# An attention kernel whose TensorE order is written out as letters, with idle products in its opening

## The chip, the cores and the metric

The kernel runs on one core of one Trainium2 chip. The metric is the device time of one execution in microseconds (us), the median of three runs.

## The reference, cut to what matters

A macaron block in float32: half a mixture of eight experts, attention, and half a mixture again, over x of 4 batches x 1024 tokens x 128 features.

```python
x = x + 0.5 * _L0_ffn_ref(_layernorm(x), Wr, br, ln_g, ln_b, W1, b1, W2, b2)
x = x + _L0_attn_ref(_layernorm(x), Wq, Wk, Wv, Wo)
x = x + 0.5 * _L0_ffn_ref(_layernorm(x), Wr, br, ln_g, ln_b, W1, b1, W2, b2)


# inside _L0_attn_ref: 16 heads of 8 features
q = split_heads(x @ Wq.T); k = split_heads(x @ Wk.T); v = split_heads(x @ Wv.T)
q = _rope(q, pos); k = _rope(k, pos)
score = jnp.einsum('bqd,bkd->bqk', q, k)
score = jnp.where(causal[None], score, -jnp.inf)
attn = jax.nn.softmax(score / jnp.sqrt(jnp.float32(D_K)), axis=-1)
out = jnp.einsum('bqk,bkd->bqd', attn, v)
return out @ Wo.T
```

## The kernel before, in words

**Stages.** Attention works in 16 stages (NST) of four heads (QH) of one batch. Queries and keys are split into three bf16 parts each and stacked, so that one product over 72 rows gives a float32 score. Each stage is done twice over: first the row maxima are found, then the scores are computed again with the maximum subtracted, through three more rows of the stack (75 rows), and exponentiated.

**The jobs on TensorE.** Each has a function.
- `tile` (L1297): scores of 128 queries against all keys up to them, into one of two PSUM buffers `psS`. There are 24 per stage: t0 to t7 hold two heads (128, 256, 384, 512 columns a head; two tiles of each), t8 to t23 one head (640, 1024, 768 and 896 columns, four of each, in this order). VectorE (`reduce`, L1448) adds the mask and takes the maximum. They are made for the stage after the one whose scores run.
- `turn_max`: turns the split maxima of one half of a stage (half 0: queries 0 to 511, the first eight tiles; half 1: the rest). GpSimd splits them before (`split`, five short steps), VectorE copies the result (`copy_max`, L1456), a DMA writes it into the stack (`load_max`).
- `score` (L1339): scores turned, of 128 keys against up to 512 queries, into one of three PSUM buffers `psST`. A stage has 12 units (u0 to u11) of four heads (s4.0 is unit 4, head 0; w4 is its weigh), of 512, 384, 256, 128, five times 512, 384, 256, 128 queries, 48 scores in all. Scores of unit 4 and later need the maxima of half 1. ScalarE's `exps` (L1412) takes the exponential.
- `weigh` (L1353): the exponentials of one unit times the values, into `psO`; for units on the diagonal GpSimd's `mask` (L1533) stands before it. ScalarE copies `psO` after units 3 and 11 (`copy_out`, L1418).
- `turn_out` (L1323): turns such a copy back, and VectorE divides by the sums (`normalise`).

**What waits for what.** The jobs `tile`, `turn_max` and `turn_out` take turns on the two buffers of `psS`: each is a use with an index, and use k waits until VectorE has read use k-2 (`use`: `wait(pe, use_read, index - 1)`). Score m waits for exponential m-3. `exps` of unit u waits for weigh u-3, since `prob` is a ring of three. In the last stage there are no tiles, and the scores use five buffers.

**The order.** TensorE works its queue in order. `plan(first, last)` computes the order of a stage: scores in order, a weigh two units behind (LAG = 2) after the first score of each unit, tiles spread by cost (`spread`), and the turns at fixed units (EXTRAS). Before the stages stands `opening()`: 12 tiles of stage 0, its first `turn_max`, four more tiles, and eight tiles with the 16 scores and 2 weighs of units 0 to 3 among them. Written with the letters that the change uses (s score, w weigh, t tile of the next stage, o tile of stage 0 in the opening, m and M the turn of half 0, N of half 1, A and B `turn_out` of half 0 and 1), the order before is:

```
opening  oooooooooooomooooossossossosssowsossoswosss
first    tttNwtttttwtssstsstsstsAswtsstsswtstssMswttsstsswtstssswtsstsswtsss
middle   swttsstsswtsstsNswtssstswssstswtssstBswtsstsAswtsstsswtstssMswttsstsswtstssswtsstsswtsss
last     swsssswsssNswsssswsssswsssBswsssAswsssswsssswsssswsssswsssswssswwB
```

VectorE and GpSimd follow the same list of uses (`uses`, `base`, `half_ready`). Ahead of attention TensorE runs products of ones (`warm_up`, L253).

Of the kernel before, what the change touches and what calls it, by code (L numbers as in the profile page):

```python
# [20 lines left out]
P = 128  # L21
# [8 lines left out]
QH = 4  # L30
# [1065 lines left out]
def attention(nc, n, ctx, block):  # L1096
# [26 lines left out]
    tile_cost = [len(heads) * (i + 1) * P + 350 for heads, i in tiles]  # L1123
    tile_total = sum(tile_cost)

    WEIGH_COST = 3
    att_total = sum((QH + WEIGH_COST) * w for _, _, _, w in units)

    def plan(first, last, whole=False):

        found, tile = [], 0
        att = sum((QH + WEIGH_COST) * w for _, _, _, w in units[:OPEN]) if first and not whole else 0

        def spread():
            nonlocal tile
            while not last and tile < MT and sum(tile_cost[:tile + 1]) * att_total <= att * tile_total + AHEAD:
                found.append(("tile", tile, 0))
                tile += 1  # L1140

        if first and not whole:
            found += [("tile", t, 0) for t in range(OPEN_TILES)]
            tile = OPEN_TILES
        for u in range(UN):
            if first and not whole and u == OPEN:
                for v in range(OPEN - LAG, OPEN):
                    found.append(("weigh", v, 0))
                    att += WEIGH_COST * units[v][3]
                    spread()  # L1150
            w = units[u][3]
            for h in range(0 if first and u < OPEN and not whole else QH):
                found.append(("score", u, h))
                att += w
                if h == 0:
                    if u >= (OPEN + LAG if first and not whole else LAG):
                        found.append(("weigh", u - LAG, 0))
                        att += WEIGH_COST * units[u - LAG][3]
                    elif u < LAG and not first:
                        found.append(("weigh", u - LAG, 1))  # L1160
                        att += WEIGH_COST * units[u - LAG + UN][3]
                spread()
            for at, what, arg, there in EXTRAS:
                if at == u and (there or not (first if arg == 1 and what == "turn_out" else last)):
                    found.append((what, arg, 0))
        att = att_total * 2
        spread()
        return found

    OPEN, OPEN_AFTER, OPEN_TILES = CB, 4, 3  # L1170

    def opening():

        head = MT // 2 + 1 + OPEN_AFTER
        found = [(what, arg, 0) for _, what, arg in before_loop[:head]]
        jobs = plan(True, True, True)
        jobs = jobs[:jobs.index(("score", OPEN, 0))]
        jobs = [job for job in jobs if job[0] in ("score", "weigh")]
        for k, (_, what, arg) in enumerate(before_loop[head:]):
            found.append((what, arg, 0))  # L1180
            a, b = (len(jobs) * i // (MT - MT // 2 - OPEN_AFTER) for i in (k, k + 1))
            found += jobs[a:b]
        return found

    def uses(first, last):

        return [(0, what, arg) for what, arg, _ in plan(first, last) if what in ("tile", "turn_max", "turn_out")]

    LAG = 2
    AHEAD = tile_total * tile_cost[0]  # L1190

    EXTRAS = [(1, "turn_max", 1, True), (4, "turn_out", 1, False), (5, "turn_out", 0, True),
              (7, "turn_max", 0, False)]
    before_loop = [(0, "tile", t) for t in range(MT // 2)] + [(0, "turn_max", 0)]
    before_loop += [(0, "tile", t) for t in range(MT // 2, MT)]
    OPENED = [arg for what, arg, _ in opening() if what == "weigh"]
    USES = len(uses(False, False))

    def base(s, first):

        return len(before_loop) if first else len(before_loop) + len(uses(True, False)) + (s - 1) * USES

    PARITY = base(1, False) % 2
    assert USES % 2 == 0

# [43 lines left out]
    def run(stage):  # L1249


        stage(0, 0, 0, True, False)
        for s in range(1, NST):
            stage(s, s % RING, s // RING, False, s == NST - 1)
# [8 lines left out]
    def _(sp):  # L1263
# [10 lines left out]
        def stage(s, r, turn, first, last):  # L1274
            if not first:
                load_max(s, r, 1)
            if not first and s + 2 < NST:
                load(s + 2, (r + 2) % RING)
            if not last:
                load_max(s + 1, (r + 1) % RING, 0)  # L1280
# [11 lines left out]
    def _(pe):  # L1292
# [4 lines left out]
        def tile(r, turn, t, index, ps):  # L1297

            heads, i = tiles[t]
            if t == 0:  # L1300
                pe.wait_ge(stack_loaded[r], (turn + 1) * 16 * STACK_DMAS)
# [24 lines left out]
        def score(s, r, u, h):  # L1326

            ch, j, q0, w = units[u]
            if u in half_start and h == 0:
# [5 lines left out]
            elif m < 5:  # L1335
                pe.wait_ge(use_read, base(s, False))
# [5 lines left out]
        def weigh(s, r, u):  # L1342

            ch, j, q0, w = units[u]
            pe.wait_ge(exp_done, s * SC + (u + 1) * QH)
# [12 lines left out]
        def stage(s, r, turn, first, last):  # L1358
            b, parity = base(s, first), base(0, True) % 2 if first else PARITY
            k = 0  # L1360
            for what, arg, arg2 in plan(first, last):
                if what == "score":
                    score(s, r, arg, arg2)
                    continue
                if what == "weigh":
                    if arg2:
                        weigh(s - 1, (r - 1) % RING, arg + UN)
                    else:
                        weigh(s, r, arg)
                    continue  # L1370
                ps = psS[(parity + k) % 2]
                if what == "tile":
                    tile((r + 1) % RING, turn + (r + 1) // RING, arg, b + k, ps)
                elif what == "turn_max":
                    turn_max(s if arg else s + 1, arg, b + k, ps)
                else:
                    turn_out(s - 1 if arg else s, arg, b + k, ps)
# [8 lines left out]
        k = 0  # L1386
        for what, arg, arg2 in opening():
            if what == "score":
                score(0, 0, arg, arg2)
            elif what == "weigh":  # L1390
                weigh(0, 0, arg)
            elif what == "tile":
                tile(0, 0, arg, k, psS[k % 2])
# [198 lines left out]
```

## Time and profile before

| what | value |
|---|---|
| runs | 857.47, 857.72, 861.70 us, median 857.72 |
| profiled execution, span | 855.6 us from its first to its last instruction |
| profiled execution, own time | not listed apart from the three runs; the median lies 2.1 us above the span |
| TensorE busy | 779.7 us (91%) |
| VectorE busy | 610.9 us (71%) |
| ScalarE busy | 507.4 us (59%) |
| GpSimd busy | 315.4 us (37%) |
| mean granted TensorE clock | 0.945 of full |

Times in the rows are counted from the start of the span. PE is TensorE, DVE VectorE, ACT ScalarE, POOL GpSimd. A product's shown duration reaches past the start of the next product, so how long one occupies the engine is read from start to start. PEclk is the granted clock as a share of 2.4 GHz; 0.50 is 1.2 GHz. Attention runs from about 202 to 714 us.

### The profile page before, as it was taken

The numbers are of one execution on the slowest core, as the hardware profiler recorded it, in microseconds if no ns is written. First come the engines' busy times: TensorE is split into PE (matmuls) and PEld (weight loads), VectorE is DVE, ScalarE is ACT, GpSimd is POOL, SyncE is SP. The second block draws the span as 40 slices with busy tenths as digits, with TensorE's granted clock in tenths as the row PEclk, the third lists the DMA queues.
The fourth block names the chain that finished last, engine by engine and source line by source line (L and its number), as shares of the span: only waits on it lengthen the run. The fifth ranks groups of instructions, "written<-read, shape, count | busy, mean of one in ns | idle before, by whom it ended". The sixth has DMA issues, their size and how long they took to land. (4 is left out here: it accounts for less than half of the span.)

```text
span 855.6 us, 17846 instructions
## 1 busy us (share of the span) xinstructions
PE 779.7 (91%) x5570; PEld 427.9 (50%) x5570; DVE 610.9 (71%) x1919; ACT 507.4 (59%) x1229; POOL 315.4 (37%) x603
## 2 busy tenths in 40 slices
PE   9889999887899999999999999999999997689995
PEld 8888896543233333333333333333333335579884
DVE  4657774698668777788878878788787722856663
ACT  2166651673247767667667766766777684146662
POOL 6177742475104223223322422331242231056753
PEclk8699999998569999999999999999999998789998
DMA  8721113065332033033113303312320001122110
GB/s 271 270 57 50 54 33 117 23 169 159 57 57 45 14 57 57 10 49 58 34 26 57 53 6 57 58 22 36 57 41 18 3 1 34 73 70 50 52 42 26
DMA packets 27989, 51.84 MB, mean 61 GB/s; under 512 B 7552, under 2 KB 19200, under 8 KB 26496
## 3 DMA queue, kind: packets, MB, share of 16 engines
q1 hardware_dynamic: 21296, 41.04, 20.7%
q0 software_dynamic: 4096, 8.69, 3.8%
q10 hardware_dynamic: 2512, 1.06, 0.5%
q8 instruction: 43, 0.70, 0.4%
q14 instruction: 42, 0.34, 0.1%
HBM read 35.40 MB, written 14.97 MB: 59 GB/s over the span
## 5 line engine op out<-in xcount | busy, mean ns | idle before, releaser
L1448 DVE CUSTOM_DVE_ANT_0 cst<-psS,mask_row 128x768 bf16<-128x768 f32 (+7 forms) x512 | 364.7, 756 | 100.2 <-PE psS L1308 97.6
L1412 ACT ACTIVATE prob<-psST 128x512 f32<-128x512 f32 (+3 forms) x750 | 317.3, 495 | 158.9 <-PE psST L1339 155.2
L1353 PE MATMUL a_psO<-prob,vs 128*32 128x512 f32 (+3 forms) x1536 | 166.7, 506 | 2.8 <-ACT prob L1412 1.7
L1532 POOL TENSOR_TENSOR a_gate<-a_zeros 1x1 f32<-1x1 f32 x128 | 23.7, 185 | 333.7 <-ACT prob L1412 333.7
L1339 PE MATMUL psST<-a_qs,ks 75*128 75x512 bf16 (+1 forms) x480 | 123.7, 327 | 5.9 <-ACT prob L1412 3.5
L1308 PE MATMUL psS<-ks,a_qs 72*128 72x512 bf16 (+2 forms) x480 | 119.0, 337 | 5.6 <-DVE a_rowmax L1448 5.5
L777 POOL DMA_INDIRECT tok<-rows,f_there_number x64 | 61.8, 966 | 86.0 <-DVE f_number L489 42.0
L1308 PEld LDWEIGHTS psS<-ks,a_qs 72*128 72x128 bf16 x480 | 35.6, 99 | 101.1 <-DVE a_rowmax L1448 33.0
L1308 PE MATMUL psS<-ks,qs 72*128 72x512 bf16 (+3 forms) x288 | 75.8, 354 | 6.7 <-DVE a_rowmax L1448 6.5
L1533 POOL TENSOR_SCALAR_AFFINE_SELECT prob<-prob 128x512 f32<-128x512 f32 x128 | 80.3, 627 | 0.0
L1339 PE MATMUL psST<-qs,ks 75*128 75x512 bf16 (+3 forms) x270 | 73.4, 346 | 2.7 <-ACT prob L1412 1.7
L1339 PEld LDWEIGHTS psST<-a_qs,ks 75*128 75x128 bf16 x480 | 43.8, 97 | 61.4 <-ACT prob L1412 28.8
L726 ACT ACTIVATE f_xnT<-f_ps_half,gb 128x128 f32<-128x128 f32 x64 | 29.3, 458 | 54.4 <-PE f_ps_half L654 54.4
L522 DVE TENSOR_SCALAR f_hidT<-f_ps_wide,f_w1s 128x128 f32<-128x128 f32 x156 | 47.2, 345 | 18.0 <-PE f_ps_logit L663 13.7
L663 PE MATMUL f_ps_wide<-f_xnT,f_w1s 128*128 x312 | 49.7, 282 | 10.0 <-ACT f_hidT L734 5.4
L743 ACT ACTIVATE f_w1s<-w 128x516 f32 x78 | 49.7, 637 | 9.8 <-DVE f_item_ring L479 9.3
L1353 PEld LDWEIGHTS a_psO<-prob,vs 128*32 128x32 f32 x1536 | 30.6, 108 | 48.1 <-ACT prob L1412 31.6
L1308 PEld LDWEIGHTS psS<-ks,qs 72*128 72x128 bf16 x288 | 21.6, 100 | 64.5 <-DVE a_rowmax L1448 28.4
L663 PEld LDWEIGHTS f_ps_wide<-f_xnT,f_w1s 128*128 128x128 f32 x312 | 40.9, 191 | 14.1 <-issue 14.0
L673 PE MATMUL f_ps_rank<-w,f_hidT 128*128 x320 | 45.4, 285 | 0.3 <-DVE f_hidT L522 0.3
L1339 PEld LDWEIGHTS psST<-qs,ks 75*128 75x128 bf16 x270 | 25.6, 102 | 38.8 <-ACT prob L1412 17.9
L1448 DVE DVE_READ_ACCUMULATOR2_ANT a_rowmax<- 128x1 f32 x512 | 42.6, 83 | 0.0
(183 smaller groups left out, 1066.1 us busy)
## 6 DMA issues: line engine op xcount, KB each, us to landing
a_qs<-q_split SPq DMA_DIRECT2D x60, 96.0 KB
rows<-tok SPq DMA_DIRECT2D x8, 536.0 KB, 4.9
ks<-k_split SPq DMA_DIRECT2D x32, 128.0 KB
qs<-q_split SPq DMA_DIRECT2D x36, 96.0 KB
q_split<-p_part SPq DMA_DIRECT2D x24, 128.0 KB, 2.4
k_split<-p_part SPq DMA_DIRECT2D x24, 128.0 KB, 2.4
ks<-k_split SPq DMA_DIRECT2D x16, 192.0 KB
tok<-x_after_first SPq DMA_DIRECT2D x4, 536.0 KB, 5.4
```

Of the source, the lines that this page charges most:

```text
L522: last = nc.vector.tensor_scalar(hidT[i % 2][:, f * P:(f + 1) * P], hidden_at(i, f), w1s[i % 4][:, F + f:F + f + 1], 0.0, ALU.add, ALU.max)
L663: last = nc.tensor.matmul(hidden_at(i, f), w1s[i % 4][:, f * P:(f + 1) * P], xnT[:, ds(slot_of[i], 1), :], start=True, stop=True)
L673: last = nc.tensor.matmul(psY[i % 2], hidT[i % 2][:, f * P:(f + 1) * P], n.w2[:, ds(expert[i], 1), f * D:(f + 1) * D], start=(f == 0), sto ...
L726: nc.scalar.activation(xnT[:, t % XR, :], psX[t % 2], ACT.Identity, bias=n.gb[:, 1:2], scale=n.gb[:, 0:1]).then_inc(x_ready, 1)
L743: nc.scalar.activation(w1s[i % 4][:, :], n.w1[:, ds(expert[i], 1), :], ACT.Copy).then_inc(w1_ready, 1)
L777: pool.indirect_dma_start(out=row[:, t, :], out_offset=None, in_=n.rows_dram[r][:, :], in_offset=bass.IndirectOffsetOnAxis(ap=there_number ...
L1308: last = nc.tensor.matmul(ps[:, a * CH + c0:a * CH + c0 + w], lhs, ks[r][0:PR, h * S + c0:h * S + c0 + w], start=True, stop=True)
L1339: nc.tensor.matmul(score_buffer(s, m)[:, 0:w], ks[r][:, h * S + j * P:h * S + (j + 1) * P], qs[r][:, q_col(h, q0):q_col(h, q0) + w], start ...
L1353: last = nc.tensor.matmul(psO[32 * h:32 * h + 32, c0:c0 + w], vs[r][:, j, h, :], prob[:, u % RING, h, 0:w], start=(j == 0), stop=(u + 1 in ...
L1412: nc.scalar.activation(prob[:, u % RING, h, 0:w], score_buffer(s, u * QH + h)[:, 0:w], ACT.Exp, scale=SCALE).then_inc(exp_done, 1)
L1448: last = nc.vector.tensor_tensor_reduce(out=out[:, a * CH:a * CH + width], in0=ps[:, a * CH:a * CH + width], in1=mask_row[:, S - width:], ...
L1533: nc.gpsimd.affine_select(out=part, in_=part, compare_op=ALU.is_ge, fill=0.0, base=0, pattern=[[0, QH], [1, P]], channel_multiplier=-1).th ...
```

## The change

`plan`, `opening`, `uses` with its cases for first and last, `before_loop` and the tail behind `run` go away. The order is three strings, one for the first, the middle and the last stage; `jobs(s)` turns letters into jobs by counting them, and all engines read their order from the same `program`. The opening is now part of the first string. New is the letter `f`: an idle product of ones, 128 rows by 512 columns, into `psO`, whose content nothing reads. There are 48, all among the 24 tiles `o` of the opening, the last two behind the last of them. `COPIES` says ahead of which unit's exponentials ScalarE copies `psO`: of this stage's first half ahead of unit 5 in the first stage and 6 otherwise (5 before), of the previous stage's second half ahead of unit 2 in middle stages and 1 in the last (1 before). A weigh still runs two units behind at the stage's border.

```diff
+    FIRST = ("offofoffoffoofoffffofffofffoffomfffofoffoffffofsfsofffsoffoffoffoffsossofsossffsoffstwtstssssNtt"
+             "wtwtsstsswsststwtstssststwstsstswtsstswMtssAsststssststsswssts")
+    MIDDLE = ("sstswtstsstswssNtstswstsstswwsstssBsstsstwstsstsstwssttsswtssAsststwssMsttsswssttssswwsts")
+    LAST = ("ssswswssssNsswssssswssssswwssssssBssswssswsssswsssswsssswssssAwww")
+    COPIES = {FIRST: (5, None), MIDDLE: (6, 2), LAST: (6, 1)}
+    OWN_MASKS = 2
+    def jobs(s):
+        seen = dict.fromkeys("swto", 0)
+        weighed = s * UN - lag(s)
+        found = []
+        for k in letters(s):
+            n = seen.get(k)
+            if n is not None:
+                seen[k] += 1
+            if k == "s":
+                found.append(("score", s, n // QH, n % QH))
+            elif k == "w":
+                found.append(("weigh", (weighed + n) // UN, (weighed + n) % UN, 0))
+            elif k in "to":
+                found.append(("tile", s + (k == "t"), n, 0))
+            elif k in "mMN":
+                found.append(("turn_max", s + (k == "M"), int(k == "N"), 0))
+            elif k in "AB":
+                found.append(("turn_out", s - (k == "B"), int(k == "B"), 0))
+            else:
+                found.append(("idle", s, 0, 0))
         return found
+    def lag(s):
+        return s * UN - sum(letters(i).count("w") for i in range(s))
+    program = [jobs(s) for s in range(NST)]
+    program[-1].append(("turn_out", NST - 1, 1, 0))
...
+                if what == "idle":
+                    nc.tensor.matmul(psO[:, :].rearrange("p (a b) -> p a b", b=P), n.onesb[:, :],
+                                     n.onesb[:, :].unsqueeze(1).to_broadcast([P, CH // P, P]), start=True, stop=True)
+                    continue
...
-                if u == 1 and not first:
+                if u == before:
                     copy_out(s - 1, 1)
-                if u == half_end[0] + 1:
+                if u == own:
                     copy_out(s, 0)
```

On GpSimd the order of stage 0 stays: split of half 0, two masks, split of half 1, then the other masks. The number of scores, tiles, weighs, turns, exponentials, masks and DMAs is the same as before.

## Rows read from the trace of the kernel before

**Rows 1.** The page: busy time, and the granted clock in 40 slices.
```profile
PE 779.7 (91%) x5570; PEld 427.9 (50%) x5570; DVE 610.9 (71%) x1919; ACT 507.4 (59%) x1229; POOL 315.4 (37%) x603
...
PEclk8699999998569999999999999999999998789998
```

**Rows 2.** Windows: length, busy PE, PEld, DVE, ACT, POOL; PEclk, DMA share, GB/s.
```profile
202.30:205.60 3.30, 2.00 (x12) 0.67 (x12) 2.79 (x17) 1.51 (x3) 3.09 (x4) 1.00 0.43 118
...
218.50:231.20 12.70, 12.70 (x47) 4.35 (x46) 7.62 (x17) 5.51 (x13) 1.58 (x4) 0.50 0.35 53
...
241.10:264.80 23.70, 22.81 (x118) 7.94 (x116) 16.48 (x36) 14.85 (x33) 3.75 (x12) 0.81 0.12 20
398.12:428.43 30.31, 28.90 (x203) 10.63 (x202) 24.17 (x70) 21.19 (x51) 8.65 (x27) 1.00 0.24 42
...
689.15:714.30 25.15, 21.89 (x173) 7.30 (x173) 1.94 (x7) 20.90 (x53) 7.98 (x23) 1.00 0.01 1
```

**Rows 3.** Timeline of ACT: copies of the weighed output.
```profile
267.87 0.60 ACT L1418 ACTIVATE p_anT<-a_psO 128x512 f32<-128x512 f32 x1
419.43 0.60 ACT L1418 ACTIVATE p_anT<-a_psO 128x512 f32<-128x512 f32 x1
```

**Rows 4.** Timeline of PE in a middle stage: start, duration, line, count.
```profile
400.24 1.06 PE L1353 MATMUL a_psO<-prob,vs 128*32 128x512 f32 x8
401.24 0.60 PE L1308 MATMUL psS<-ks,qs 72*128 72x512 bf16 x2
...
408.04 0.60 PE L1339 MATMUL psST<-a_qs,ks 75*128 75x512 bf16 x2
408.94 0.50 PE L1308 MATMUL psS<-ks,qs 72*128 72x512 bf16 x2 [0.30 <-DVE a_rowmax L1448]
...
415.67 0.33 PE L1339 MATMUL psST<-a_qs,ks 75*128 75x128 bf16 x3
416.35 0.38 PE L1339 MATMUL psST<-qs,ks 75*128 75x512 bf16 x1 [0.35 <-ACT prob L1412]
...
420.63 0.22 PE L1316 MATMUL psS<-identb,a_maxparts 128*128 128x128 bf16 x1
...
424.77 0.38 PE L1339 MATMUL psST<-qs,ks 75*128 75x512 bf16 x1
...
427.94 0.43 PE L1353 MATMUL a_psO<-prob,vs 128*32 128x128 f32 x8
428.29 0.45 PE L1308 MATMUL psS<-ks,a_qs 72*128 72x512 bf16 x2
```

**Rows 5.** Timeline of DVE and ACT in the same middle stage.
```profile
405.86 1.22 DVE L1448 CUSTOM_DVE_ANT_0 cst<-psS,mask_row 128x1024 bf16<-128x1024 f32 x1
408.80 0.08 DVE L1448 DVE_READ_ACCUMULATOR2_ANT a_rowmax<- 128x1 f32 x1
421.37 0.21 DVE L1456 COPY a_maxT<-psS 48x128 bf16<-48x128 bf16 x1
402.10 2.06 ACT L1412 ACTIVATE prob<-psST 128x512 f32<-128x512 f32 x4 [0.93 <-PE psST L1339]
```

**Rows 6.** Timelines of the opening: DVE, POOL and PE.
```profile
232.14 0.09 DVE L1448 DVE_READ_ACCUMULATOR2_ANT a_rowmax<- 128x1 f32 x1
232.31 0.22 POOL L1511 TENSOR_TENSOR a_maxparts<-a_zeros,a_rowmax 128x16 bf16<-128x16 f32 x1 [7.26 <-DVE a_rowmax L1448]
233.87 0.26 PE L1316 MATMUL psS<-identb,a_maxparts 128*128 128x128 bf16 x1 [0.56 <-POOL a_maxparts L1516]
241.11 1.49 PE L1339 MATMUL psST<-qs,ks 75*128 75x512 bf16 x3
```

**Rows 7.** Timeline of PE, and windows, while products of ones run.
```profile
744.76 4.33 PE L253 MATMUL f_ps_spare<-onesb 128*128 128x128 bf16 x44
...
745.00:746.00 1.00, 1.00 (x12) 1.00 (x11) 0.89 (x4) 0.00 (x0) 0.00 (x0) 0.50 0.98 394
...
748.00:749.00 1.00, 1.00 (x16) 0.92 (x14) 1.00 (x3) 0.51 (x1) 0.00 (x0) 0.83 1.02 416
```

More of the change, by code:

```diff
@@ L1120, in attention @@
     MT = len(tiles)
[L1123 to L1167, printed above, removed]
-        return found
@@ L1170, in attention @@
[L1170 to L1196, printed above, removed]
@@ new lines, in lag, with base, read_by @@
+    def lag(s):
+        return s * UN - sum(letters(i).count("w") for i in range(s))
+    program = [jobs(s) for s in range(NST)]
+    program[-1].append(("turn_out", NST - 1, 1, 0))
+    uses = [[(what, of, arg) for what, of, arg, _ in found if what in ("tile", "turn_max", "turn_out")]
+            for found in program]
+    def base(s):
+        return sum(len(found) for found in uses[:s])
+    def read_by(s, half):
+        everything = [use for found in uses for use in found]
+        return max(k for k, use in enumerate(everything)
+                   if use[0] == "tile" and use[1] == s and (use[2] >= HALF_TILES) == (half == 1)) + 1
@@ L1249, in run @@
     def run(stage):
-        stage(0, 0, 0, True, False)
-        for s in range(1, NST):
-            stage(s, s % RING, s // RING, False, s == NST - 1)
+        for s in range(NST):
+            stage(s)
     def score_buffer(s, m):
@@ L1272, in load_max, with stage @@
             sp.dma_start(max_rows(r, half), maxT[half][:, :]).then_inc(max_loaded[half], 16)
[L1274 to L1280, printed above, removed]
+        def stage(s):
+            if s > 0:
+                load_max(s, s % RING, 1)
+            if s > 0 and s + 2 < NST:
+                load(s + 2, (s + 2) % RING)
+            if s + 1 < NST:
+                load_max(s + 1, (s + 1) % RING, 0)
         load_max(0, 0, 0)
@@ L1385, in _ @@
         pe.wait_ge(n.v_copied, NC8)
[L1386 to L1393, printed above, removed]
-                k += 1
-            else:
-                turn_max(0, arg, k, psS[k % 2])
-                k += 1
         run(stage)
-        weigh(NST - 1, (NST - 1) % RING, UN - 2)
-        weigh(NST - 1, (NST - 1) % RING, UN - 1)
-        end = base(NST - 1, False) + len(uses(False, True))
-        turn_out(NST - 1, 1, end, psS[end % 2])
     @block.scalar
@@ L1418, in copy_out, with stage @@
             nc.scalar.activation(outT[:, :], psO[:, :], ACT.Copy).then_inc(out_copied, 1)
-        def stage(s, r, turn, first, last):
+        def stage(s):
+            own, before = COPIES[letters(s)]
             for u in range(UN):
-                if u == 1 and not first:
+                if u == before:
                     copy_out(s - 1, 1)
-                if u == half_end[0] + 1:
+                if u == own:
                     copy_out(s, 0)
@@ L1534, in mask, with stage @@
                                     pattern=[[0, QH], [1, P]], channel_multiplier=-1).then_inc(masked, 1)
-        def stage(s, r, turn, first, last):
-            for u in diagonal[len(OPENED) if first else 0:]:
-                if u == half_end[0] + CB:
-                    if not last:
-                        split(s + 1, 0, base(s, first) + half_ready["first" if first else "middle", 0],
-                              2 * s + 2)
-                        values(s + 1, (r + 1) % RING)
+        def stage(s):
+            for at, u in enumerate(diagonal):
+                if s == 0 and at == OWN_MASKS:
+                    split(0, 1)
+                if u == half_end[0] + CB and s + 1 < NST:
+                    split(s + 1, 0)
+                    values(s + 1, (s + 1) % RING)
                 mask(s, u)
-            if not last:
-                split(s + 1, 1, base(s, first) + half_ready["first" if first else "middle", 1], 2 * s + 3)
+            if s + 1 < NST:
+                split(s + 1, 1)
         pool.wait_ge(cleared, 1)
```

82 lines of the change are left out of this document (33 added, 49 removed).

## The prediction

> **What bounds the kernel now.** I read the page's head first: TensorE (PE) is busy 91% of the span, and PEclk is below full in three places, one of them the slices from 214 to 257 us (digits 5 and 6), where attention opens [rows 1]. Then a table of windows over attention [rows 2]: the granted clock is full to 205.6 us, half (.50) from there on, back to full inside 241.1 to 264.8 (.81 over it), full in a middle stage. Up to 205.6 VectorE (DVE) is busy 2.79 of 3.30 us and TensorE waits for it; in 218.5 to 231.2 TensorE has no gap at all (12.70 of 12.70), at half speed, and everything waits for it. Third, ScalarE's copies of the weighed output (L1418), two a stage, mark the stages [rows 3]; the window of 30.31 us from 398.12 to 428.43 lies between two of the same kind and is one middle stage. There are fourteen, all alike. Last, TensorE in order of time over a middle stage [rows 4]: a "busy" of 28.90 of 30.31 hides waits, for a product's shown duration runs past the start of the next.
>
> What must TensorE do in a middle stage? Starts give the durations. The 18432 columns of scores take .22 us per 512 (two from 408.04 to 408.48, 7.9 us in all with the narrow ones); the tiles of maxima are as many columns, .44 for a 1024-wide one, 8.0 in all; a weigh of 512 takes 1.00 (400.24 to 401.24), one of 128 .36 (427.94 to 428.29), those of 384 and 256 on a line between, 9.4 per stage [rows 4]. I put the four transposes at 1.2 (the tail of a stage's list, an estimate). A score directly ahead of a weigh takes .31 in place of .22, and 12 weighs have one: 1.1. Sum 27.6; the remaining 2.7 are waits. Rows show the two largest: the score pair from 408.04 is through at 408.48, but the next tile starts at 408.94, .14 after the accumulator read at 408.80; three 128-wide scores from 415.67 (.17 of work) hold the engine to 416.35 [rows 4, 5]. The rest are .05 to .4 each.
>
> **The change, part by part.** *Middle order (14 stages).* Counts stay: 48 scores, 24 tiles, 12 weighs, three kinds of transposes. Nothing is cheaper, only who waits. I walked the 88 letters with the durations above, 1.15 us of DVE for a 1024-wide tile (1.22, of which the next one covers .07) and less for narrower, .49 of ScalarE (ACT) for a 512-wide exponential [rows 5], .14 from the accumulator read to the next tile, and three score buffers. Work is 27.14, since only 7 weighs now follow a score (5 times .09 less); the waits that I find are small: .1 before s0.2 (an exponential), .1 before t3, .2 before t4 (the read of t3), and seven of under .1 in the part where ACT runs without a break. The old places of waiting are covered: t16 comes after w5, and between t17 and t18 stand A, two scores and s8.3; the narrow scores of unit 11 have w8, w9 and t23 among them. Moved waits: the two `w` behind each other (w1 w2) need mask 2, which POOL has some .4 us before; `s10.0` ahead of w7 makes ACT wait 1 us for buffer space, with ACT idle there anyway; copy_out one unit later falls behind wp11, which TensorE has then issued. The first wide score stands 4.8 us of TensorE work behind N, where the chain N, copy, DMA takes 4.1 (420.63 to 424.77) [rows 4]. Walk: 27.9. I take 28.2, adding .3 for what coarse durations hide. Bounds: no wait at all 27.1; nothing won 30.3. That is 14 times 2.1, 29.5 us.
>
> DVE (24.17 a stage) and ACT (21.19) [rows 2] stay under 28.2; a period of 27 would already put DVE at .9.
>
> By the Trainium skill (Trainium Kernel Development and Optimization, section Best Practices) matmul busy is no measure of how near TensorE is to its limit. The trace agrees: the starts sum to 27.6 under a busy of 28.90. Who took busy as work would allow 1.4 us per stage, 19.7 in all, and come out near 823.
>
> *The opening.* Removed is the half clock. 48 idle products of 512 columns stand between the 24 tiles `o`. At full clock each takes .22, so 10.4 us; with tiles (8.0) and eleven early scores (1.8) TensorE has 20.3 us of work. DVE needs 22.8 for the 24 reads and a copy (a middle stage's 24.17 less two normalisations of .6, less one copy). DVE begins at 202.7 and is the busier engine from the start (2.79 to 2.00 [rows 2]), so idle products only fill TensorE's waits if the clock holds. Going tile by tile, the `m` after o10 waits for POOL's split, free at 211.2, and costs DVE .6. The last read ends at 225.5 instead of 232.14 [rows 6]. From there: the split on POOL and N 1.7 later (232.31 and 233.87 now), at 227.2, copy to 227.7, 3.1 for the DMA of maxima (copy ends 421.58, wide score 424.77) [rows 4, 5]: first wide score of stage 0 at 230.8, now 241.11 [rows 6]. TensorE's own letters in between (t3 to t6, w1, w2; 2.7 us from 227.2) end sooner, so about 1 us of waiting is in it. The stack for stage 1 is issued on SyncE's queue behind the first maxima, new about 1.2 us earlier than now; t0 stands at 224.6, some 12 after it. A stack is 11 pieces, 1.2 MB; I expect it late by a few tenths at most, and add nothing. If it were late, t0 and with it DVE's next tile would wait for it.
>
> From the wide score to stage 1: 17 tiles, 32 scores, seven weighs and A are 19.0 us of work at full clock; with waits 20.3. Stage 1 would start at 251.1. Now it starts 3.1 us before its copy at 267.87 (as 416.35 stands before 419.43), at 264.8, because the stretch is at .81 [rows 2, 3]. Gain 13.7.
>
> At half clock the same opening is 40.5 us of TensorE work: that is the bound on the other side. Which end? Rows speak both ways. Before the drop TensorE was busy 2.00 of 3.30 us [rows 2]; in middle stages, where waits are 9% of the time, it is 1.00 [rows 2], slice after slice [rows 1]. Products of the same ones ran from 744.76 when the clock came back from half (745) to full, in 748 to 749 [rows 7]. Against: 12.7 us without a gap at half clock, 218.5 to 231.2, brought nothing back. Holding is not regaining, so I take full clock.
>
> The Trainium skill (TensorE: Matmul & The Clock Gate, section What's actually happening) says activity lifts the throttle. The stretch to 231.2 goes against the simple reading, and there the row decides. By the rule alone the opening's gain would be certain.
>
> *Last stage.* 25.15 us now [rows 2]. Weighs are two units later, so the first wide exponentials aren't behind w1 and mask 2; units 0 to 3 take ACT 5.2 us (four each of .49, .39, .25 and .17) and a copy .5, the maxima have landed at 6.3 (N at 2.7 and 3.6 more), so they begin at 6.8. From there ACT has 13.5 us (20 wide, 12 narrow, a copy), then a tail of about 3 for a mask, w11, copy and transpose: 23.3, and 23.45 with a little waiting. Gain 1.7, bounds 0 and 2.5.
>
> Sum: 13.7 + 29.5 + 1.7 = 44.9 off the span of 855.6 is 810.7. The median of the runs lies 2.1 above the span, so 813.
>
> **Rivals.**
> (A) The clock falls again around N, where TensorE waits about 2 us of 6.4 (as much idle time as ahead of 205.6). Half clock for the 10 to 14 us that follow costs 5 to 7: 818 to 820.
> (B) The idle products don't hold the clock. For: rows 2's gapless half-clock stretch. Opening 40.5 us, o23 near 241, the wide score 7 on at 248, then 23.7 as now [rows 2]: stage 1 at 272 rather than 251.1, 813 + 21 = 834.
> (C) The new middle order waits elsewhere as much as the old one: 813 + 29.5 = 842. For it speaks that ACT and DVE both get near saturation from s4.0 to t17, where one late event is passed on; against, each old wait has a cover in the new letters.
> (D) Slower: the clock drops in the middle stages. Place: a wait in each, such as N's chain running past the 4.8 us. Price: a microsecond at half clock loses half a microsecond of TensorE work. It decides once 44.9/14 = 3.2 us are lost per stage, 6.4 us at half clock in each; twice that gives about 903. Against: the clock row of the page shows no dip in all middle stages [rows 1], with larger waits than the walk has.
> (E) The letters amount to nothing: clock lost as in B and most of C's waits back as well; 855 to 863.
>
> **Numbers.** Forecast .57 (own range 804 to 822, from periods 27.6 to 28.8), A .15, B .13, C .08, D .04, E .03. Range 804 to 836: it takes in A and B and leaves C, D, E and a period under 27.6, together under .2. A measurement here tells .5% (4 us) from nothing. Faster: forecast, A, B, C less a little, .92; same .03; slower .05.
>
> **What would show it.** Copies of ScalarE 28.2 apart rather than 30.31; PEclk full in the slices from 214 to 257; last read of the opening near 225.5; the first wide score near 231; stage 15 in 23.5. Wrong if the copies stand 30 apart, if the idle products take .43 each, or if DVE's opening is stretched by them.

## The result, and the profile after

The changed kernel takes 801.08 us (median of 4 runs, 798.72 to 803.22); the kernel before takes 859.71 beside it (4 runs, 857.47 to 862.26). The ratio is 0.9329, with a 95% interval of 0.9294 to 0.9364. Medians and ranges are over all executions of a kernel, ratios over those within 1.5% of its fastest. Forecast were 813 us and a range of 804 to 836: the direction and the mechanism came as forecast, the gain is 12 us larger, and the time lies 2.9 us below the range.

The page of the changed kernel, which answers to [rows 1]: busy times and the granted clock.

```profile
PE 751.4 (94%) x5618; PEld 438.9 (55%) x5618; DVE 609.3 (76%) x1919; ACT 506.8 (63%) x1229; POOL 313.9 (39%) x603
...
PEclk8599999999999999999999999999999999689998
```

TensorE has 48 instructions more, the idle products, and is busy 28.3 us less; the other engines do what they did. The dip of the clock at 214 to 257 us is gone.

Windows of the changed kernel, for those of [rows 2]: where the clock was full before its fall; where the old kernel ran without a gap at half clock; from the first wide score of stage 0 (the first one of unit 4, which needs the maxima of half 1) to stage 1; one middle stage; all fourteen; the last stage. The columns are those of [rows 2].

```profile
201.90:205.60 3.70, 3.51 (x20) 1.55 (x20) 3.16 (x19) 1.63 (x3) 3.50 (x4) 1.00 0.47 127
218.50:231.20 12.70, 12.40 (x80) 4.86 (x78) 12.17 (x42) 5.43 (x15) 4.13 (x13) 1.00 0.37 69
229.84:249.53 19.69, 19.69 (x128) 6.99 (x127) 18.13 (x42) 14.64 (x32) 3.73 (x12) 1.00 0.33 54
385.77:413.02 27.25, 27.25 (x205) 11.09 (x203) 24.14 (x70) 21.17 (x51) 8.57 (x27) 1.00 0.26 46
249.53:631.03 381.50, 381.50 (x2830) 155.34 (x2829) 338.03 (x982) 296.40 (x701) 120.01 (x378) 1.00 0.24 43
631.03:654.60 23.57, 22.01 (x175) 7.43 (x172) 2.42 (x7) 20.68 (x52) 7.93 (x23) 1.00 0.01 2
```

The clock is full in all of them. A middle stage takes 27.25 us for 30.31, and there is no variation: 381.50 is 14 times 27.25. 

Timeline of TensorE in the changed kernel: the last tile of the opening, N (L1292), the first wide score of stage 0, the first score of stage 1, and two places of a middle stage where two weighs (L1331, x16) stand behind each other.

```profile
223.25 0.54 PE L1284 MATMUL psS<-ks,qs 72*128 72x512 bf16 x2
...
226.66 0.22 PE L1292 MATMUL psS<-identb,a_maxparts 128*128 128x128 bf16 x1
...
229.84 0.60 PE L1316 MATMUL psST<-qs,ks 75*128 75x512 bf16 x2
...
249.53 0.59 PE L1316 MATMUL psST<-a_qs,ks 75*128 75x512 bf16 x2
...
392.75 1.28 PE L1331 MATMUL a_psO<-prob,vs 128*32 128x384 f32 x16
393.97 0.45 PE L1316 MATMUL psST<-qs,ks 75*128 75x128 bf16 x2
...
410.86 1.71 PE L1331 MATMUL a_psO<-prob,vs 128*32 128x512 f32 x16
412.50 0.23 PE L1316 MATMUL psST<-qs,ks 75*128 75x128 bf16 x1
```

N comes at 226.66 rather than 233.87, the first wide score at 229.84 rather than 241.11 [rows 6], and no product of the stretch from 385.77 to 413.02 names a releaser (an event of another engine that it waited for), where the middle stage before has several [rows 4].

The balance in the two profiled executions (spans 855.6 and 799.6, a difference of 56.0):

| part | before | after | gain | forecast |
|---|---|---|---|---|
| up to stage 1 | 264.8 | 249.53 | 15.3 | 13.7 |
| 14 middle stages | 424.3 | 381.5 | 42.8 | 29.5 |
| last stage | 25.15 | 23.57 | 1.6 | 1.7 |
| after attention | 141.3 | 145.0 | -3.7 | 0 |

The last row is no effect of the order. The windows from the end of attention to the end of the program, first of the kernel before, then of the changed one, have the same instructions but for one, and a lower clock in the second:

```profile
714.30:855.60 141.30, 114.24 (x939) 105.36 (x939) 87.06 (x355) 62.98 (x160) 62.83 (x64) 0.90 0.17 52
```

```profile
654.60:799.60 145.00, 117.56 (x940) 108.17 (x939) 87.11 (x355) 62.98 (x160) 62.75 (x64) 0.88 0.17 51
```

In the profiled executions of the kernels below with the same last stage, it took 141.4 (`old_first`), 141.7 (`no_idle`), 142.6 (`half_idle`), 144.8 (`early_idle`), 144.9 (`split_ww`) and 145.2 us (`pairs_all`): it varies from execution to execution, and so does the part ahead of attention (VectorE takes the first tile at 202.38 in the changed kernel, at 205.46 in `split_ww`).

### The profile page after: what moved, and what is told of

Same layout as the page of the kernel before. It is cut to its first block and busy times, and to the rows that moved or that the text cites. A ratio compares the mean times of both kernels' runs of the same rounds, so it can differ in the third digit from the quotient of the medians.

```text
span 799.6 us, 17942 instructions
## 1 busy us (share of the span) xinstructions
PE 751.4 (94%) x5618; PEld 438.9 (55%) x5618; DVE 609.3 (76%) x1919; ACT 506.8 (63%) x1229; POOL 313.9 (39%) x603
## 3 DMA queue, kind: packets, MB, share of 16 engines
q10 hardware_dynamic: 2512, 1.06, 0.5%
## 5 line engine op out<-in xcount | busy, mean ns | idle before, releaser
L1331 PE MATMUL a_psO<-prob,vs 128*32 128x512 f32 (+3 forms) x1536 | 157.5, 496 | 0.4 <-ACT p_anT L1380 0.2
L1316 PE MATMUL psST<-a_qs,ks 75*128 75x512 bf16 (+1 forms) x480 | 125.8, 328 | 0.0
L1284 PE MATMUL psS<-ks,a_qs 72*128 72x512 bf16 (+2 forms) x480 | 112.4, 326 | 0.1
L1316 PE MATMUL psST<-qs,ks 75*128 75x512 bf16 (+3 forms) x270 | 71.8, 328 | 0.1
L1284 PE MATMUL psS<-ks,qs 72*128 72x512 bf16 (+3 forms) x288 | 67.8, 327 | 0.6 <-DVE a_rowmax L1411 0.3
L1331 PEld LDWEIGHTS a_psO<-prob,vs 128*32 128x32 f32 x1536 | 34.1, 108 | 57.3 <-ACT prob L1374 28.8
L1284 PEld LDWEIGHTS psS<-ks,a_qs 72*128 72x128 bf16 x480 | 40.4, 97 | 42.1 <-DVE a_rowmax L1411 21.1
L1316 PEld LDWEIGHTS psST<-qs,ks 75*128 75x128 bf16 x270 | 24.0, 97 | 46.1 <-ACT prob L1374 30.4
L790 POOL DMA_INDIRECT out_x<-tok,f_number x32 | 32.0, 1000 | 25.2 <-DVE tok L545 20.5
```

What stands on the lines that cost most here:

```text
L790: pool.indirect_dma_start(out=target, out_offset=bass.IndirectOffsetOnAxis(ap=number[:, t:t + 1], axis=0), in_=row[:, t, 0:TW if r == 0 el ...
L1316: nc.tensor.matmul(score_buffer(s, m)[:, 0:w], ks[r][:, h * S + j * P:h * S + (j + 1) * P], qs[r][:, q_col(h, q0):q_col(h, q0) + w], start ...
L1331: last = nc.tensor.matmul(psO[32 * h:32 * h + 32, c0:c0 + w], vs[r][:, j, h, :], prob[:, u % RING, h, 0:w], start=(j == 0), stop=(u + 1 in ...
```

## The experiments

Each changes only strings or the tuple of the copies in the changed kernel; where a fence shows the first line of `FIRST` alone, the rest of the string stays. Where the middle stage is compared, the marks are the copies of the weighed output on ScalarE. Half clock means a granted clock of .50.

**What the parts are worth.** `old_middle` has the middle stages as they were, with their copies:

```diff
-    MIDDLE = ("sstswtstsstswssNtstswstsstswwsstssBstsstwstsstsstwssttsswtssAsststwssMsttsswssttssswwsts")
-    COPIES = {FIRST: (5, None), MIDDLE: (6, 2), LAST: (6, 1)}
+    MIDDLE = ("swttsstsswtsstsNswtssstswssstswtssstBswtsstsAswtsstsswtstssMswttsstsswtstssswtsstsswtsss")
+    COPIES = {FIRST: (5, None), MIDDLE: (5, 1), LAST: (6, 1)}
```

> The changed kernel with the middle stages in the order of the kernel before, letter for letter, and its places of ScalarE's copies. Theory: the middle order is worth 14 times 3.06 us: copies 30.3 apart again, median about 801 + 43 = 844. Rival: part of the shorter stage comes from the state in which the new opening leaves the engines, so that the old letters run at 28 to 29: 811 to 825.

Measured: 846.16 us (842.87 to 850.07), ratio to the kernel before 0.9837 (0.979 to 0.9883), stages of 30.31 us. It is 45.1 above the changed kernel, as the theory had it; the middle stages alone account for 42.8.

`old_first` has the old opening and first stage, without idle products, and the new middle and last stages:

```diff
-    FIRST = ("offofoffoffoofoffffofffofffoffomfffofoffoffffofsfsofffsoffoffoffoffsossofsossffsoffstwtstssssNtt"
-             "wtwtsstsswsststwtstssststwstsstswtsstswMtssAsststswststsswssts")
+    FIRST = ("oooooooooooomooooossossossosssowsossoswosss"
+             "tttNwtttttwtssstsstsstsAswtsstsswtstssMswttsstsswtstssswtsstsswtsss")
```

> The changed kernel with the first stage and its opening in the order of the kernel before and without idle products; middle and last letters are the new ones. Theory: the opening and first stage are worth 62.5 - 47.6 = 15 us from the first tile to the start of stage 1, of which the idle products give 5.9 and the order 9: median 801 + 15 = 816. Rival: the parts overlap (with the old order the half clock ends elsewhere), 808 to 812.

Measured: 814.06 us (812.68 to 814.4), ratio 0.9469 (0.9427 to 0.951): the new opening and first stage are worth 13.0 us (the theory had 15). The two parts, 45.1 and 13.0, make 58.1 of the 58.6 us between the kernels.

**What the idle products are worth.** `no_idle` leaves all 48 out and keeps the new order. `half_idle` keeps 24, spread over the whole opening; `early_idle` keeps the 20 that stand ahead of `m`.

```diff
-    FIRST = ("offofoffoffoofoffffofffofffoffomfffofoffoffffofsfsofffsoffoffoffoffsossofsossffsoffstwtstssssNtt"
+    FIRST = ("ooooooooooomoooossosoooosossososssostwtstssssNtt"   # no_idle
+    FIRST = ("ofofofofoooffoffofofomffoofoffofssoffsofofofofsossosossfsofstwtstssssNtt"   # half_idle
+    FIRST = ("offofoffoffoofoffffofffofffoffomoooossosoooosossososssostwtstssssNtt"   # early_idle
```

> The changed kernel without its 48 idle products; every other letter stays. Theory: the idle products hold the clock, and that is the whole gain of the opening. Then the clock falls near 205.6 us as in the kernel before, TensorE works through the opening's tiles and first scores at half clock, stage 1 starts near 264 us as before instead of 249.5, and the median is about 801 + 14 = 815. Rival: the new order of letters alone shortens the opening, the clock matters little since VectorE sets the pace there: 801 to 804.

Measured: 809.93 us (806.55 to 817.33), ratio 0.9456 (0.939 to 0.9521). The windows of this kernel, from its first tile to the fall, to the return, to stage 1:

```profile
204.70:207.50 2.80, 1.69 (x10) 0.56 (x10) 2.29 (x15) 1.16 (x3) 2.59 (x3) 0.94 0.37 102
207.50:237.90 30.40, 27.45 (x93) 7.80 (x92) 25.10 (x75) 6.97 (x18) 8.55 (x22) 0.50 0.46 101
237.90:258.20 20.30, 20.30 (x134) 7.21 (x130) 18.35 (x44) 14.65 (x32) 3.73 (x12) 1.00 0.26 42
```

The clock does fall, for 30 us, but it is back where the wide scores begin (238.49). From its first tile to stage 1 this kernel takes 53.5 us, the changed one 47.6, the one before 62.5. So in these executions the idle products are worth 5.9 us of the opening and its order 9.0. By the medians the idle products are worth more, 8.9 us: the profiled execution (806.76 us) is one of the two short ones of four, the others took 813.10 and 817.33. The windows say why the loss is small here: at half clock, TensorE with no idle products to run is busy 27.45 us of the 30.40, and VectorE, which has to read every tile, 25.10, so the clock takes little beyond what VectorE needs. I had expected the whole gain of the opening to go with the clock, and stage 1 near 264 us; it starts at 258.2, and that theory fell.

> The changed kernel with every second idle product left out, 24 of 48. Theory: the clock goes by how much of the time TensorE works; with half of them it works about 75% of the time, more than in the stretch where the clock fell (61% by busy time), and the clock holds; the distance from the first tile to the copy of stage 0's first half stays 30.3 or loses a few tenths, 801. Rival: the clock falls as without them: 35 to 36 us, 806.

Measured: 801.63 us (799.23 to 803.67), ratio 0.9335 (0.9309 to 0.9361), as with 48, and the clock is full throughout; here TensorE is busy 16.27 of the first 19.7 us (window of this kernel), so the clock stands more idleness than the changed kernel leaves:

```profile
202.30:222.00 19.70, 16.27 (x74) 5.34 (x74) 18.77 (x58) 5.26 (x10) 8.04 (x14) 1.00 0.66 150
```

> The changed kernel with the 20 idle products ahead of the first turn of maxima, and none behind it. Theory: TensorE's share of work without them is about 60% later too, so the clock falls some microseconds behind the turn, near 215, and the opening is about as long as without any: 5 us longer than the changed kernel's, 806 to 808 (as the distance between the first tile and the copy of stage 0's first half: 35 to 36 us, 30.3 in the changed kernel, 36.2 without any). Rival: what the clock needs is only not to fall in the first tiles; once the 1024-wide tiles and scores run it stays full: 30 to 31 us, 801.

Measured: 809.74 us (806.36 to 819.39), ratio 0.9408 (0.9372 to 0.9444), not told apart from no idle product at all (809.93), as the theory had it. The profiled execution is the longest of the four, 819.39 us. Its windows: the first half of the opening, from the fall to the first wide score, and behind that:

```profile
203.00:214.00 11.00, 9.22 (x48) 3.74 (x48) 10.05 (x42) 2.22 (x4) 7.30 (x12) 1.00 0.61 167
214.40:236.37 21.97, 20.92 (x77) 6.57 (x77) 17.03 (x49) 6.34 (x16) 4.21 (x13) 0.50 0.41 77
236.37:260.00 23.63, 23.63 (x82) 6.23 (x80) 12.81 (x28) 11.11 (x20) 1.44 (x6) 0.50 0.18 31
```

The clock falls at 214.3, behind the last idle product, so the second half of the opening needs them as well. Here it is back only at 262.1, though TensorE has no gap in 23.63 us of that: the way from the first wide score to stage 1 takes 31.5 us for 19.7. So these two kernels without idle products in the second half differ in how long the half clock lasts in the profiled executions, 30 and 48 us, and with it in what the idle products save: 5.9 us from the first tile to stage 1 against `no_idle`, 17.2 against this one. Why it lasts longer here isn't shown.

**The rival of the prediction at N.** `idle_only` has the old letters everywhere, the copies (5, None), (5, 1) and (5, 1), and 43 idle products in its opening, here against the opening before:

```diff
-    FIRST = ("oooooooooooomooooossossossosssowsossoswosss"
+    FIRST = ("offofoffoffoofoffffofffofffoffofffofmoffoffffoffofffoffssoffssoffssoffsssowsossoswosss"
```

> The order of the kernel before in all stages, with 43 idle products among the tiles of its opening (as many behind each tile as in the changed kernel, none once the first weigh has begun to write the same bank). Theory: the clock holds through the opening, first wide score of stage 0 near 231 instead of 241, stage 1 near 251: median about 859 - 14 = 845. Rival: the old opening has no early scores between its tiles and waits at its end, so the clock falls anyway and each idle product costs .43 us: 865 to 870.

Measured: 855.11 us (852.12 to 863.48, 10 runs), ratio 0.9969 (0.9935 to 1.0004): a gain of 3.3 us at the median, not told apart from nothing, where the theory had 14 and the rival a loss. Windows of this kernel around N:

```profile
226.00:228.00 2.00, 1.15 (x13) 0.58 (x9) 2.00 (x7) 0.61 (x3) 0.05 (x1) 1.00 0.00 0
228.00:230.00 2.00, 0.81 (x5) 0.24 (x5) 1.75 (x13) 0.00 (x0) 1.69 (x7) 1.00 0.01 4
230.00:232.00 2.00, 1.29 (x12) 0.50 (x12) 0.77 (x5) 0.00 (x0) 0.83 (x3) 0.87 0.09 18
232.00:234.00 2.00, 1.80 (x4) 0.26 (x4) 1.97 (x10) 0.00 (x0) 0.00 (x0) 0.50 0.85 180
```

The idle products hold the clock to 231.5; the old order lets TensorE stand idle around N (3.25 us busy of 6), and the clock falls for 14 us. This is rival A, and in the changed kernel the letters prevent it: from 226.66 to 229.84 its TensorE runs tiles and weighs, and the profile shows no gap. In the profiled execution of `idle_only` the first wide score comes 32.8 us behind the first tile, for 38.8 before, and from there to stage 1 it takes 23.8 for 23.7. So in this execution the idle products win 6.0 us under the old letters too, and what they don't win is the stretch from the first wide score on, 19.7 in the changed kernel. Idle products without the order, or the order without idle products, each leave a half-clock stretch.

**The middle stage: paired weighs.** `split_ww` puts a score between the two weighs of both pairs; `pairs_all` pairs two others as well (w6 w7 and w10 w11).

```diff
-    MIDDLE = ("sstswtstsstswssNtstswstsstswwsstssBstsstwstsstsstwssttsswtssAsststwssMsttsswssttssswwsts")
+    MIDDLE = ("sstswtstsstswssNtstswstsstswswstssBstsstwstsstsstwssttsswtssAsststwssMsttsswssttsswswsts")   # split_ww
+    MIDDLE = ("sststswwtsstsssNtstswstsstswwsstssBstsstwstsstsstwssttsswtssAsststswwsMsttssssttssswwsts")   # pairs_all
```

> The changed kernel with one score moved between the two weighs that stand behind each other, at both places of a middle stage. Theory: two weighs in a row save some .15 us between them and a second .09 of a weigh that follows a score, so each place is worth about .24 and 14 stages with two places 6.7: period 27.7, median 808. Rival: the saving only looks so in the trace or is taken back by a wait: period 27.2 to 27.4, 801 to 803.

Measured: 811.96 us (811.42 to 816.0), ratio 0.9467 (0.9425 to 0.9509). A stage takes 27.74 us, .49 more, as the theory had it (27.7); timeline of ScalarE in this kernel, two copies of one kind:

```profile
376.62 0.59 ACT L1379 ACTIVATE p_anT<-a_psO 128x512 f32<-128x512 f32 x1
...
404.35 0.59 ACT L1379 ACTIVATE p_anT<-a_psO 128x512 f32<-128x512 f32 x1
```

14 times .49 are 6.9 of the 9.8 us between the spans of the two profiled executions (809.4 and 799.6); 3.1 are the later first tile of this one. In the changed kernel the pair from 392.75 (384 and 256 wide) takes 1.22 us, where the line between [rows 4] gives 1.36, and the one from 410.86 (512 and 384) 1.64 for 1.79. So a pair saves some .15, and besides one entry into a weigh (a product directly ahead of a weigh holds TensorE some .09 us longer). Of the 3.06 us won per stage the two pairs are .49; the rest is waits.

> The changed kernel with two more pairs of weighs behind each other in a middle stage: 10 with 11 and 6 with 7. Theory: as with the pairs that are there, each saves about .24 us where no wait takes it back: period 26.8, median 795. Rival: TensorE is the bound but VectorE (24.1 us a stage) and ScalarE (21.2) are starved for two microseconds behind each pair, and a wait takes the saving back: period 27.2 or more, 801 to 805.

Measured: 824.11 us (819.61 to 829.58), ratio 0.9594: slower than with two pairs. A stage takes 28.71 us at full clock. Timeline of TensorE in this kernel, where it waits again:

```profile
361.74 0.28 PE L1315 MATMUL psST<-a_qs,ks 75*128 75x256 bf16 x1 [0.36 <-ACT prob L1373]
...
362.69 0.55 PE L1283 MATMUL psS<-ks,a_qs 72*128 72x512 bf16 x2 [0.28 <-DVE a_rowmax L1410]
...
366.84 0.28 PE L1283 MATMUL psS<-ks,qs 72*128 72x128 bf16 x2 [0.37 <-DVE a_rowmax L1410]
```

The first two stand 2.0 and 3.0 us behind the pair of 1.9 us that w6 and w7 make there (357.87 to 359.73). The third is t1, which in the changed kernel has w10 ahead of it and here follows two scores and t0; its pair, w10 w11, comes only behind it, at 367.27. My reading is that ScalarE and VectorE run out of scores and tiles during a long pair and are late afterwards, and that VectorE isn't through with its last tile where a weigh no longer covers it; this isn't shown, for the two new pairs weren't run one by one.

**The middle stage: the copies.** The prediction costed `COPIES` at nothing. Three kernels keep the new letters and move one copy or both to the old unit, and one has the old letters with the new copies:

```diff
-    COPIES = {FIRST: (5, None), MIDDLE: (6, 2), LAST: (6, 1)}
+    COPIES = {FIRST: (5, None), MIDDLE: (5, 1), LAST: (6, 1)}     # copies_old
+    COPIES = {FIRST: (5, None), MIDDLE: (5, 2), LAST: (6, 1)}     # own_copy_early
+    COPIES = {FIRST: (5, None), MIDDLE: (6, 1), LAST: (6, 1)}     # prev_copy_early
```

```diff
-    MIDDLE = ("sstswtstsstswssNtstswstsstswwsstssBstsstwstsstsstwssttsswtssAsststwssMsttsswssttssswwsts")
+    MIDDLE = ("swttsstsswtsstsNswtssstswssstswtssstBswtsstsAswtsstsswtstssMswttsstsswtstssswtsstsswtsss")   # old_letters_new_copies
```

> The changed kernel with ScalarE's copies in middle stages back at their old places (ahead of units 5 and 1 instead of 6 and 2); the letters stay. Theory: the later weighs need the later copies. The copy of the previous stage then stands in ScalarE's queue ahead of unit 1 but can only run behind weigh 11, which TensorE issues some 3.3 us into the stage, so unit 1's exponentials start about 1 us late and TensorE's scores with them: period 28 to 28.5, median 812 to 818. Rival: the copies' places don't matter, since ScalarE is idle for 6 of 27 us: period 27.25, 801.

> The changed kernel with only ScalarE's copy of a middle stage's own first half back ahead of unit 5 (new: unit 6). With both copies back a stage took 29.66 us at full clock and 34.2 where the clock dipped. Theory: this copy alone costs a wait of .6 us at the fifth unit, period about 28.1 at full clock; one such wait a stage is too little for the clock to dip: 801 + 12 = 813. Rival: one lumped wait is enough, and the clock dips in part of the stages: 830 or more.

> The changed kernel with only ScalarE's copy of the previous stage's second half back ahead of unit 1 (new: unit 2). Theory: it costs the wait of 1.1 us ahead of the fifth score pair, period about 28.8 at full clock, and being longer than the other it is what makes the clock dip: 822 if the clock holds, 845 to 865 if it dips in most stages. Rival: only both together do it: 822.

> The changed kernel with the middle letters of the kernel before but the new places of ScalarE's copies. Theory: letters and copies belong together; with a weigh two units behind, the later copies hold up the next write of the bank instead, and the period stays near 30.3: 844 to 848. Rival: the places of the copies are a good part of the 3.06 us by themselves: period 28 to 29.3, 815 to 832.

| middle letters | copies | us | shortest stage |
|---|---|---|---|
| new | (6, 2) | 801.08 | 27.25 |
| new | (5, 2) | 834.15 (825.95 to 839.93) | 28.42 |
| new | (6, 1) | 848.28 (842.17 to 855.93) | 28.49 |
| new | (5, 1) | 876.11 (871.19 to 883.79) | 29.66 |
| old | (5, 1) | 846.16 (842.87 to 850.07) | 30.31 |
| old | (6, 2) | 907.92 (893.98 to 928.5) | 34.05, none at full clock |

Timelines of `copies_old`, ScalarE first, then TensorE, show one stage:

```profile
402.50 0.60 ACT L1379 ACTIVATE p_anT<-a_psO 128x512 f32<-128x512 f32 x1 [0.70 <-PE a_psO L1330]
...
422.75 0.60 ACT L1379 ACTIVATE p_anT<-a_psO 128x512 f32<-128x512 f32 x1 [0.81 <-PE a_psO L1330]
```

```profile
403.64 0.88 PE L1315 MATMUL psST<-a_qs,ks 75*128 75x512 bf16 x2 [0.61 <-ACT prob L1373]
...
423.79 0.67 PE L1315 MATMUL psST<-qs,ks 75*128 75x384 bf16 x2 [1.10 <-ACT prob L1373]
```

In the old letters w11 stands behind s1.0 and w3 behind s5.0; in the new ones behind s1.2 and s5.1. A copy ahead of the exponentials of unit 5 or 1 stands at the head of ScalarE's queue and waits .70 or .81 us for that weigh; the exponentials behind it, for which everything is ready, wait too, and TensorE then waits .61 or 1.10 for their buffers, and a little more at the scores behind. With a copy one unit later the weigh is done when its turn comes: in the changed kernel no copy of a middle stage names a releaser. At full clock the two losses simply add: 28.42 has 1.17 over 27.25, 28.49 has 1.24, and both together, 29.66, have 2.41.

The second part of the cost is the clock. Windows of `copies_old` in the stage before that one:

```profile
386.00:388.00 2.00, 2.00 (x19) 0.88 (x18) 1.92 (x13) 1.75 (x4) 1.68 (x7) 1.00 0.02 4
388.00:390.00 2.00, 0.90 (x11) 0.27 (x10) 0.84 (x6) 1.43 (x4) 0.66 (x2) 0.92 0.00 0
390.00:392.00 2.00, 2.00 (x9) 1.02 (x8) 1.05 (x4) 1.36 (x4) 0.77 (x2) 0.50 0.00 0
...
398.00:400.00 2.00, 2.00 (x13) 0.65 (x6) 0.00 (x0) 0.83 (x2) 0.68 (x2) 0.52 0.84 143
400.00:402.00 2.00, 2.00 (x13) 1.07 (x11) 1.92 (x5) 1.62 (x4) 1.49 (x7) 1.00 0.50 80
```

In this stage the wait of 1.10 us ends with the scores at 389.60:

```profile
389.60 0.78 PE L1315 MATMUL psST<-a_qs,ks 75*128 75x384 bf16 x2 [1.10 <-ACT prob L1373]
```

By its .92 over 388 to 390 the clock falls some .1 us behind that, and TensorE runs ten gapless microseconds at half speed before it is back. That stage takes 34.19. In the profiled execution (span 881.8) the waits are 14 times 2.41, 33.7 of the 82.2 us above the changed kernel's. The rest, 48.5, lies where the clock is half: of the thirteen distances from one copy ahead of unit 5 to the next, two are 29.66 at full clock, and the other eleven, 31.24 to 36.74, make 48.3 us more. So the copies taken back by themselves turn the gain of 58 us into a loss of 16: ratio 1.0174 (1.0123 to 1.0225) to the kernel before. For (6, 1) the waits are 17.4 of 47.5 us, for (5, 2) 16.4 of 24.6.

The single copies settle whether one wait per stage is enough for the clock to fall. For (6, 1), with the wait of 1.10 us, it falls in all of these distances but one, as the theory had it. For (5, 2) I had expected no fall; the rival had 830 us or more, and 834.15 bears it out. In its profiled execution, the shortest of six, the clock falls in three of them, the first time 1.5 us behind the wait, at 437.2. TensorE there, and windows of a stage without a fall and of this one:

```profile
435.74 0.88 PE L1315 MATMUL psST<-a_qs,ks 75*128 75x512 bf16 x2 [0.61 <-ACT prob L1373]
```

```profile
320.92:349.34 28.42, 27.71 (x203) 11.04 (x202) 24.15 (x71) 21.15 (x50) 8.59 (x27) 1.00 0.26 44
434.60:467.85 33.25, 32.54 (x203) 11.86 (x202) 24.41 (x71) 21.26 (x51) 8.59 (x27) 0.85 0.22 38
```

With the old letters the late copies are wrong in the other way, and by more than either theory had (844 to 848, or 815 to 832). Timeline of TensorE in that kernel:

```profile
302.25 0.63 PE L1298 MATMUL psS<-cst,p_anT 128*128 128x128 f32 x4 [1.54 <-ACT p_anT L1379]
...
324.56 1.85 PE L1330 MATMUL a_psO<-prob,vs 128*32 128x512 f32 x8 [0.88 <-ACT p_anT L1379]
```

The old `A` stands right behind s5.3, and the copy that it turns is now made behind all exponentials of unit 5; the old w0 stands behind s2.0 and needs `psO`, which the late copy frees behind those of unit 1. Each waits, and all of TensorE's queue with it. The clock stays full behind the wait of 1.54 us and falls behind that of .88:

```profile
302.00:304.00 2.00, 1.75 (x13) 0.64 (x13) 0.55 (x2) 0.70 (x2) 0.00 (x0) 1.00 0.00 0
324.00:326.00 2.00, 1.45 (x8) 0.19 (x8) 0.36 (x3) 0.69 (x2) 0.76 (x2) 0.68 0.02 6
326.00:328.00 2.00, 2.00 (x10) 0.89 (x7) 0.80 (x3) 0.59 (x3) 0.00 (x0) 0.50 0.80 183
```

So in the 3.74 us by which its shortest stage is longer than one of `old_middle`, there are both the waits, 2.42 us, and what some 3 us at half clock cost.

## Why the prediction missed the range

**The step that failed** is the walk over the 88 letters: work 27.14, waits .76, and .3 added "for what coarse durations hide", 28.2. Measured is 27.25, just inside the stated bounds (27.1 to 30.3) and under my own range of periods (27.6 to 28.8): the cause was right, the size of this term was not. The term was 14 times 2.1 = 29.5 and is 14 times 3.06 = 42.8; the 13.3 us between them are more than the whole miss of the span (11.1). From the starts of the changed kernel's stage the work is 7.88 for tiles, 7.95 for scores, 9.14 for weighs, 1.0 for turns and .92 for ten entries into a weigh (.092 each): 26.9. That leaves .35 of waits where I had put 1.06, and this is most of the .95 by which 28.2 was too long. I had summed ten waits of .2 us and less that I had worked out from durations rounded to a tenth, and added .3 on top, which pointed to the wrong side. The rows name no releaser for any of them; the starts still show the larger ones: N at 389.29 holds TensorE .19 us for .06, and the score at 395.39 .33 for .22, where I had waits of .2 ahead of t4 and of under .1. The work was .24 too high, which is errors that partly cancel: I gave each pair of weighs the price of two single ones (.28 too much for both) and .2 and .12 too much to turns and tiles, but counted an entry for seven weighs where ten have one, since the three behind a tile pay it as well (.28 too little).

**The opening** came as forecast, 15.3 for 13.7, and step by step: last read of VectorE 225.0 (forecast 225.5), N 226.66 (227.2), first wide score 229.84 (230.8), from there to stage 1 19.69 (20.3, again too many waits), idle products at full clock. The stack for stage 1 delayed nothing. But its gain isn't the clock's alone, as "Removed is the half clock" had it: with the half clock left in, the profiled execution of `no_idle` still keeps 9.0 of it.

**Last stage**: 23.57 us for 23.5.

**Behind attention** I forecast nothing, and the 3.7 us given back there lie in the variation.

**The rivals.** A (the clock falls around N) happens in `idle_only`, and so with the old letters; B (idle products don't hold the clock) fell: they do, and half of them do. C (the new order waits elsewhere) didn't happen in the changed kernel, but does in orders near it (`copies_old`, `pairs_all`). D (the clock falls in the middle stages, from a wait in each) I gave .04, for the page shows no dip with the larger waits of the old order [rows 1]. In the changed kernel it stays away, but `copies_old` is this rival with its price: one wait of 1.10 us, or of .61 in `own_copy_early`, was followed by half clock in many stages, though not in all, where 2.7 us per stage in pieces of which the profile names none over .35 never were.

**Costed at nothing**: "copy_out one unit later falls behind wp11, which TensorE has then issued" was right, and I didn't say what it would cost if the cover were gone. It costs 75 us, more than any term of the sum.

**Busy time and work** differed by 1.3 us a stage before (28.90 to 27.6). The changed kernel's rows show a busy of 27.25 of 27.25 with 26.9 of work, so the two now agree within .35 us.

## What to carry to other kernels

Where several engines follow one order written by hand, an operation that waits at the head of an in-order queue is part of that order: move it with the letters, by asking which event it waits for and what stands ready behind it. Judge a wait by its size in one piece as well as by its sum, since one of .6 or 1.1 us could here cost ten microseconds of half clock behind it. Price an operation by what stands ahead of it, and count those places. A walk with rounded durations overstated the small waits here, and the stage came out .35 us above its work; that isn't a rule for every order, for `pairs_all` has less work still and takes 28.71.

## What the runs showed of the hardware that I had not expected

- In `copies_old` the clock fell right behind a wait of 1.10 us and was half for ten gapless microseconds (390 to 400), though in the next stage the same wait left it full. In `own_copy_early` it fell in three stages behind a wait of .61 us. In `old_letters_new_copies` a wait of 1.54 us left it full, and one of .88 in the same stage was followed by half clock; a stage of 34.10 us there (301.48 to 335.58) is at .95, some 3 us of half clock. What decides on the fall, beyond a wait in one piece, stays open.
- Work without a gap didn't bring the clock back at once: in the profiled execution of `early_idle` it returned at 262.1, after at least 23.63 us without a gap, and in `no_idle` after 30.4 us at half clock. What decides on the return stays open as well.
- Two weighs in a row (16 products, 32 columns wide) take some .15 us less than two apart, besides one entry: a 512-wide score directly ahead of a weigh holds TensorE .31 us and otherwise .22, and a tile the same.
- 24 idle products of 512 columns among the tiles (202.4 to 223.7) hold the clock as well as 48 (801.63 and 801.08 us), with TensorE busy 16.27 of the first 19.7 us; 20 in the first half of the opening alone don't (809.74).
